# Layer 1 stores its transposed context, and layer 2 computes keys and values from it in bf16 parts and sums values in fp32

## The chip, the core and the metric

The kernel runs on one core of a Trainium2 chip. Its engines are TensorE (PE, matrix products; its weight loads are listed as PEld), VectorE (DVE), ScalarE (ACT), GpSimd (POOL) and SyncE (SP), which here does nothing but issue transfers. Each engine runs its own list of instructions in order, and they wait for one another by semaphores. The metric is the time on the device of one execution of the whole program, in microseconds (us). TensorE's clock has two levels, 1.2 and 2.4 GHz; a granted clock of 1.00 in a row is the higher one.

## The reference

Four layers work on x of 32 batches x 56 tokens x 128 features, each an attention and a feed-forward part. All four attentions read the same context, 32 x 1500 x 128. The change concerns layers 1 and 2. In layer 1, `n_all` and `m_all` of the kernel are products of these weights, so that scores are taken against the context itself:

```python
def _L1_xattn_ref(x, context, mask, Wq, Wkv, Wout, bout):     # 16 heads of 64
    k, v = jnp.split(context @ Wkv, 2, axis=-1)
    dots = jnp.einsum('bhnd,bhmd->bhnm', q, k) * SCALE - (1.0 - mask)[:, None, :, None] * MASK_NEG
    out = jnp.einsum('bhnm,bhmd->bhnd', softmax(dots), v)
```

Layer 2 has a causal self attention (called L2a in the kernel) and then an attention of its result over the 1500 context rows (L2b), both with 16 heads of 8:

```python
def _mha(xk, xv, xq, Wk, Wv, Wq, Wo, bo, masked):
    K = jnp.einsum('bse,hed->bhsd', xk, Wk)
    V = jnp.einsum('bse,hed->bhsd', xv, Wv)
    Q = jnp.einsum('bqe,hed->bhqd', xq, Wq)
    scores = jnp.einsum('bhqd,bhkd->bhqk', Q, K)
    ...
    att = jax.nn.softmax(scores / jnp.sqrt(sk), axis=-1)
    out = jnp.einsum('bhqk,bhkd->bhqd', att, V)
    ...
    return jax.nn.relu(out @ Wo + bo)
a = _mha(inputs, inputs, inputs, Wk1, Wv1, Wq1, Wo1, bo1, masked=True)
a = _layernorm(inputs + a, g1, b1)
c = _mha(context_seq, context_seq, a, Wk2, Wv2, Wq2, Wo2, bo2, masked=False)
```

## The kernel before

Constants: B = 32 batches, S = 56 tokens, H = 16 heads, HQ = 896 = 16 x 56 columns of queries, KEYS = 1500, cut into KT = 12 tiles of KP = 125 rows. A value "in bf16 parts" is stored as its bf16 rounding (high part) and the bf16 of what is left (low part); a product of two such values is taken as three bf16 products, high x high, high x low and low x high, summed in PSUM.

**Layer 1, `heads_attention` (L1487).** The batches go by pairs, a pair in 14 tiles of 128 query rows. SP (L1568 on) loads the context of a batch into one of two buffers `ctx`. PE turns it in units `keys_n` and `keys_b` (three per batch, 500 keys each); ACT copies a turned unit as bf16 into `ct_hi`, and GpSimd or DVE writes the rest into `ct_lo`. The table `PLAN` sets in which tile each unit stands: `keys_b` in tiles 0, 1 and 3, `keys_n` of the next pair in 7, 8 and 11. The transposed context in parts is thus made here, used for the scores (L1616 to L1618) and written over.

**Layer 2, self attention, `self_attention` (L2159).** Beside its own work on 56 tokens this function prepares, one batch after the other, the keys and values of the context for L2b. `UNITS` lists nine units per batch: three `turn` units (four transposes each, L2283, copied by ACT into `ctxT`), three `keys` units (one fp32 matmul of 500 columns, L2287) and three `values` units (four fp32 matmuls of 128 columns, L2291). They use two PSUM banks `L2a_u0` and `L2a_u1` in turn. Of a key or value unit ACT copies the high part (L2390), then DVE writes the low part (`rest`, L2506), and only then the bank is free. SP's list per batch is a context load (L2250), the store of the keys (L2252, 128 partitions) and that of the values (L2254, 125 partitions); there are three context buffers and two of each output. ACT waits before the first copy of a batch for the store of two batches ago. `body` writes out the order of the units among the pieces of the self attention: scores L2301, transposes L2310, weighted sums L2320, output L2329 and L2333.

**Layer 2, attention over the context, `narrow_heads_attention` (L1835), called L2b.** A batch is 12 tiles of 125 keys, and a tile has three slots. Per tile PE computes the scores of two halves of the heads (L1978, two matmuls of 224 columns each, into bank `score0` and `score1`), and the weighted sums of the tile before (`weighted`, L1994): 20 bf16 matmuls in five groups of four. The four of a group write to four different sets of 32 columns of PE (`tile_position`), one for each group of four heads; the five groups are values high x probabilities high, high x low, low x high, and a block of ones with either part, for the sums that divide the result. ACT takes the exponential of each half (L2049) as fp32; its upper 16 bits are read as the high part, and the low part is a subtraction of 125 x 896 by GpSimd (L2075) in ten tiles and by DVE (L2115) in tiles 4 and 9. There are four buffers of probabilities.

The softmax needs the maximum of every head and query over all 1500 keys ahead of the exponential. So the scores are also computed one batch ahead with the queries as rows (12 units `max`, L1959, two matmuls of 500 columns each), DVE reduces each (L2095), and the negated maxima are turned (`negmax`, L1963) and stand as further rows below the query, so that the score matmul subtracts them. The table that sets the order:

```python
MAXSLOT = (0, 3, 5, 8, 11, 13, 16, 19, 22, 24, 27, 30)
PLAN = [(MAXSLOT[n], "max", n, f"m{n % 2}", 1) for n in range(MAXU)]
PLAN += [(6, "query", 0, "u", 2), (9, "out", 0, "u", -1), (18, "negmax", 0, "u", 1), (33, "negmax", 1, "u", 1)]
```

An entry is a slot (0 to 35 of a batch), a kind, its number, the PSUM banks, and for which batch it works, counted from the current one. The maxima use two pairs of banks, `m0` and `m1`, in turn. A query (L1952) is written by ACT in four scalings, one for each head of a group (L2038), and DVE (L2087) makes its low part. `normalise` (L2123 to L2133) on DVE, after slot 1 of the next batch, reads the sums and divides. A prologue computes queries 0 and 1 and the twelve maxima of batch 0. SP loads per batch three transfers of keys and one of values, three batches deep.

## Time and profile before

| | |
|---|---|
| median of 3 runs | 4553.55 us (4531.95 to 4565.99) |
| profiled execution | 4542.79 us, span 4541.0 us |
| TensorE busy | 3775.3 us, 83% |
| VectorE busy | 2624.2 us, 58% |
| ScalarE busy | 1900.2 us, 42% |
| GpSimd busy | 1083.1 us, 24% |
| granted TensorE clock, mean | 0.864 |
| transfers | 229.33 MB, mean 51 GB/s |

These shares are means over the whole span, in which stages with quite different limits follow each other: layer 1's attention, L2a and L2b, of which the change speaks, are three of them. The rows further down are therefore taken by stretch. All times in them are us from the span's start. A matmul's row gives its stationary operand's shape ahead of the moving one's, and matmuls overlap each other, so the distance between two starts tells the pace and the duration does not. In brackets stands how long the engine was idle ahead of the instruction, and what released it.

### The profile page before, as it was taken

How to read it: one execution, taken by the hardware profiler on the slowest of the kernel's cores; microseconds unless marked ns; L12 is line 12 of the kernel's file. 1: busy time of each engine (PE TensorE's matmuls, PEld its weight loads, DVE VectorE, ACT ScalarE, POOL GpSimd, SP SyncE). 2: the span in 40 equal slices, each digit the busy share in tenths (PEclk: the TensorE clock that was granted, in tenths of full speed). 3: DMA queues.
4: the chain of work that ended last, by engine and by line, in shares of the span. 5: the costliest groups of instructions: out<-in, count | busy, mean ns of one | idle time of the engine just before them, and what ended most of it. 6: DMA issues, size and time to landing. Idle time of an engine off the chain costs nothing. (4 is left out here: it accounts for less than half of the span.)

```text
span 4541.0 us, 85060 instructions
## 1 busy us (share of the span) xinstructions
PE 3775.3 (83%) x33810; PEld 2685.8 (59%) x33810; DVE 2624.2 (58%) x4699; ACT 1900.2 (42%) x3513; POOL 1083.1 (24%) x615
## 2 busy tenths in 40 slices
PE   6969978999999999998898957788888885346878
PEld 4644446887788877886576744555555553224544
DVE  2443335766666766675354447776667673646635
ACT  1412214555555555554254423444444441105515
POOL 0000001111111111110111104555556561005506
PEclk7979987999999999999899977876778786568979
DMA  4620000000000000000144423222222210006401
GB/s 76 129 46 34 0 20 28 22 22 16 22 15 22 15 22 22 15 15 6 59 174 168 164 100 81 69 52 69 53 62 59 67 38 6 0 15 121 83 2 30
DMA packets 150594, 229.33 MB, mean 51 GB/s; under 512 B 10295, under 2 KB 113988, under 8 KB 149956
## 3 DMA queue, kind: packets, MB, share of 16 engines
q1 hardware_dynamic: 150212, 223.91, 17.8%
q8 instruction: 280, 4.59, 0.4%
q14 instruction: 102, 0.84, 0.1%
HBM read 173.81 MB, written 50.07 MB: 49 GB/s over the span
## 5 line engine op out<-in xcount | busy, mean ns | idle before, releaser
L2075 POOL TENSOR_TENSOR L2b_plo<-L2b_p 125x896 bf16<-125x896 f32 x320 | 581.7, 1829 | 488.9 <-ACT L2b_p L2049 442.0
L1779 DVE TENSOR_SCALAR_CACHE_REDUCE L_p<-L_score,L_cols 128x1500 f32<-128x1500 f32 x224 | 398.6, 1780 | 383.6 <-PE L_score L1618 383.6
L1718 ACT CAST L_pthi<-L_pt 125x512 bf16<-125x512 f32 x672 | 350.2, 594 | 541.1 <-PE L_pt L1627 541.1
L2049 ACT ACTIVATE L2b_p<-L2b_score 125x448 f32<-125x448 f32 x768 | 389.3, 542 | 427.8 <-PE L2b_score L1978 426.2
L1638 PE MATMUL L_acc<-L_chi,L_pthi 125*128 125x128 bf16 x2688 | 462.0, 219 | 0.4 <-DVE L_attn L1799 0.4
L1640 PE MATMUL L_acc<-L_chi,L_ptlo 125*128 125x128 bf16 x2688 | 461.6, 219 | 0.0
L1639 PE MATMUL L_acc<-L_clo,L_pthi 125*128 125x128 bf16 x2688 | 461.5, 219 | 0.0
L2095 DVE TENSOR_REDUCE L2b_max<-L2b_m 112x1 f32<-112x1000 f32 x256 | 306.5, 1198 | 242.4 <-PE L2b_m L1959 240.3
L1792 DVE TENSOR_TENSOR L_ptlo<-L_pt,L_pthi 125x512 bf16<-125x512 f32 x672 | 417.9, 677 | 1.1 <-ACT L_pthi L1718 1.1
L1978 PE MATMUL L2b_score<-L2b_qst,L2b_kst 100*125 100x224 bf16 x1536 | 326.0, 324 | 85.9 <-ACT L2b_p L2049 85.1
L1702 ACT ACTIVATE L_p<-L_p,L_least 128x1500 f32<-128x1500 f32 x224 | 350.4, 1564 | 7.2 <-DVE L_p L1779 5.2
L1627 PEld LDWEIGHTS L_pt<-ident,L_p 128*125 128x125 f32 x2688 | 328.5, 188 | 31.7 <-ACT L_p L1702 1.2
L1978 PEld LDWEIGHTS L2b_score<-L2b_qst,L2b_kst 100*125 100x125 bf16 x1536 | 213.6, 170 | 223.4 <-ACT L2b_p L2049 133.0
L1627 PE MATMUL L_pt<-ident,L_p 128*125 128x128 f32 x2688 | 330.2, 273 | 0.5 <-ACT L_p L1702 0.4
L1959 PE MATMUL L2b_m<-L2b_kst,L2b_qst 96*112 96x500 bf16 x768 | 293.8, 472 | 5.2 <-DVE L2b_max L2095 4.7
L1994 PE MATMUL L2b_acc<-L2b_p,L2b_vin 125*32 125x224 bf16 x3072 | 223.1, 310 | 71.7 <-DVE L2b_plo L2115 55.3
L1616 PE MATMUL L_score<-L_cthi,L_qhi 128*128 128x500 bf16 x672 | 255.6, 380 | 21.6 <-issue 13.7
L1638 PEld LDWEIGHTS L_acc<-L_chi,L_pthi 125*128 125x128 bf16 x2688 | 263.9, 98 | 0.6 <-DVE L_attn L1799 0.6
L1639 PEld LDWEIGHTS L_acc<-L_clo,L_pthi 125*128 125x128 bf16 x2688 | 263.1, 98 | 1.4
L1640 PEld LDWEIGHTS L_acc<-L_chi,L_ptlo 125*128 125x128 bf16 x2688 | 262.7, 98 | 0.0
L1617 PE MATMUL L_score<-L_ctlo,L_qhi 128*128 128x500 bf16 x672 | 253.9, 378 | 0.0
L1618 PE MATMUL L_score<-L_cthi,L_qlo 128*128 128x500 bf16 x672 | 253.5, 377 | 0.0
(548 smaller groups left out, 7276.2 us busy)
## 6 DMA issues: line engine op xcount, KB each, us to landing
L2b_kst<-L_keys SPq DMA_DIRECT2D x96, 375.0 KB, 5.6
L_ctx<-dram_ctx SPq DMA_DIRECT2D x32, 750.0 KB
L2a_ctx<-dram_ctx SPq DMA_DIRECT2D x32, 750.0 KB
L_keys<-L2a_kout SPq DMA_DIRECT2D x32, 750.0 KB, 19.6
L_values<-L2a_vout SPq DMA_DIRECT2D x32, 750.0 KB
L2b_vin<-L_values SPq DMA_DIRECT2D x32, 750.0 KB
L0x_ctx<-dram_ctx SPq DMA_DIRECT2D x32, 672.0 KB
L3x_ctx<-dram_ctx SPq DMA_DIRECT2D x32, 672.0 KB
```

The costliest lines, as they stand in the source:

```text
L1627: m = pe.transpose(pt_ps[j][0:KP, t * 128:(t + 1) * 128], probs[k % 2][:, (4 * j + t) * KP:(4 * j + t + 1) * KP], c["ident"][:, :])
L1638: pe.matmul(acc, pt_hi[k % 2][:, t, :], c_hi[half][:, t, :], start=(t == 0), stop=False)
L1639: pe.matmul(acc, pt_hi[k % 2][:, t, :], c_lo[half][:, t, :], start=False, stop=False)
L1640: m = pe.matmul(acc, pt_lo[k % 2][:, t, :], c_hi[half][:, t, :], start=False, stop=(t == KT - 1))
L1702: act.activation(probs[k % 2][:, :], probs[k % 2][:, :], ACT.Exp, bias=least[:, k:k + 1], scale=-1.0, accum_out=total[:, k:k + 1]).then_in ...
L1718: act.copy(pt_hi[k % 2][:, 4 * j:4 * j + 4, :], pt_ps[j][0:KP, :].rearrange("p (t q) -> p t q", t=4)).then_inc(hi_done, 1)
L1779: dve.tensor_scalar(probs[k % 2][:, :].rearrange("p (i n) -> p i n", i=3), score_ps[:, :].rearrange("p (i n) -> p i n", i=3)[:, :, 0:500], ...
L1792: dve.tensor_tensor(pt_lo[k % 2][:, 4 * j:4 * j + 4, :], pt_ps[j][0:KP, :].rearrange("p (t q) -> p t q", t=4), pt_hi[k % 2][:, 4 * j:4 * j ...
L1978: m = pe.matmul(score_ps[half][0:KP, (g % 2) * GW:(g % 2 + 1) * GW], k_stack[b % RK][:, g, t * KP:(t + 1) * KP], q_top[b % RK][:, g * GW:( ...
L2049: act.activation(probs[t % RP][:, half * 2 * GW:(half + 1) * 2 * GW], score_ps[half][0:KP, 0:2 * GW], ACT.Exp).then_inc(exp_done, 1)
L2075: pool.tensor_tensor(p_lo[t % RP][:, :], probs[t % RP][:, :], p_hi[t % RP], ALU.subtract).then_inc(lo_pool, 1)
L2095: dve.tensor_reduce(max3[:, p, 0:1], v, AX.XY, ALU.max).then_inc(free[f], 1)
```

## The change

**Layer 1.** `ct_hi` and `ct_lo` become the two halves of one buffer, and SP stores it, 128 partitions x 3000 bf16, once per batch into a new DRAM tensor `L1_ct`. ACT waits for that store before it writes the buffer again. The context loads are written out around the stores.

```diff
-        ct_hi = [sp_.sb(f"{name}_cthi{i}", [128, KEYS], BF16) for i in range(2)]
-        ct_lo = [sp_.sb(f"{name}_ctlo{i}", [128, KEYS], BF16) for i in range(2)]
+        ct = [sp_.sb(f"{name}_ct{i}", [128, 2, KEYS], BF16) for i in range(2)]
+        ct_hi, ct_lo = [t[:, 0, :] for t in ct], [t[:, 1, :] for t in ct]
...
+                def store(b, buf, units_done):
+                    sp.wait_ge(unit_free, units_done)
+                    sp.dma_start(ct_dram[b], ct[buf][:, :, :]).then_inc(ct_stored[buf], 16)
+                def second(p, base, first=False):
+                    store(2 * p + 1, 1, base + place("keys_b", 2, first) + 1)
+                def third(p, base, first=False):
+                    store(2 * p + 2, 0, base + place("keys_n", 2, first) + 1)
...
-                with sp.Fori(1, PAIRS) as pair:
-                    sp.wait_ge(ctx_split, 4 * pair - 2)
-                    load(2 * pair, 0)
-                    sp.wait_ge(ctx_split, 4 * pair)
-                    load(2 * pair + 1, 1)
...
+                with sp.Fori(1, PAIRS - 2) as p:
+                    second(p, unit_base(p))
+                    sp.wait_ge(ctx_split, 4 * p + 4)
+                    load(2 * p + 3, 1)
+                    third(p, unit_base(p))
+                    sp.wait_ge(ctx_split, 4 * p + 6)
+                    load(2 * p + 4, 0)
...
+                            if k == 0:
+                                wait(act, ct_stored[buf], 16 * (p + 1 - buf))
```

**Layer 2, self attention.** It loads the stored transposed context instead of the context, so the three `turn` units are gone, and the weights are split into bf16 parts once. A key unit is three bf16 matmuls of 500 columns, a value unit twelve bf16 matmuls of 128 columns. Values are stored as fp32 by one copy of ACT, without DVE; keys are stored in parts as before. The load of batch b + 3 is issued behind the two stores of batch b.

```diff
-        UNITS = [("turn", 0), ("turn", 1), ("keys", 0), ("turn", 2), ("keys", 1), ("values", 0), ("keys", 2),
-                 ("values", 1), ("values", 2)]
+        UNITS = [("keys", 0), ("values", 0), ("keys", 1), ("values", 1), ("keys", 2), ("values", 2)]
...
+        ct = [sp_.sb(f"{name}_ct{k}", [128, 2, KEYS], BF16) for k in range(RC)]
...
-                    if b + RC < B:
-                        sp.wait_ge(*freed(b, UNITS.index(("turn", 2))))
-                        sp.dma_start(ctx[b % RC][:, :, :], ctx_dram[b + RC]).then_inc(ctx_loaded[b % RC], 16)
                     sp.wait_ge(*freed(b, UNITS.index(("keys", 2))))
                     sp.dma_start(k_dram[b], k_out[b % 2][:, :, :]).then_inc(k_stored[b % 2], 16)
                     sp.wait_ge(*freed(b, UNITS.index(("values", 2))))
-                    sp.dma_start(v_dram[b], v_out[b % 2][:, :, :]).then_inc(v_stored[b % 2], 16)
+                    sp.dma_start(v_dram[b], v_out[b % 2][:, :]).then_inc(v_stored[b % 2], 16)
+                    if b + RC < B:
+                        sp.dma_start(ct[b % RC][:, :, :], ct_dram[b + RC]).then_inc(ct_loaded[b % RC], 16)
...
+                    if kind == "keys":
+                        ps, third = u_ps[f][:, 0:TK], slice(j * TK, (j + 1) * TK)
+                        pe.matmul(ps, cw_hi[:, 0, :], t_hi[:, third], start=True, stop=False)
+                        pe.matmul(ps, cw_hi[:, 0, :], t_lo[:, third], start=False, stop=False)
+                        m = pe.matmul(ps, cw_lo[:, 0, :], t_hi[:, third], start=False, stop=True)
...
+                            ps, tile = u_ps[f][0:KP, t * D:(t + 1) * D], slice((4 * j + t) * KP, (4 * j + t + 1) * KP)
+                            pe.matmul(ps, t_hi[:, tile], cw_hi[:, 1, :], start=True, stop=False)
+                            pe.matmul(ps, t_hi[:, tile], cw_lo[:, 1, :], start=False, stop=False)
+                            m = pe.matmul(ps, t_lo[:, tile], cw_hi[:, 1, :], start=False, stop=True)
```

ACT's and DVE's part of a unit (ACT now has six copies per batch where it had nine, DVE three subtractions where it had six):

```diff
-                    act.copy(out_part(kind, j, b, 0), unit_part(kind, f)).then_inc(hi_done, 1)
+                    if kind == "keys":
+                        act.copy(key_part(j, b, 0), u_ps[f][:, 0:TK]).then_inc(hi_done, 1)
+                    else:
+                        act.copy(v_out[b % 2][:, j * 4 * D:(j + 1) * 4 * D], u_ps[f][0:KP, 0:4 * D]).then_inc(u_free[f], 1)
...
-                    dve.tensor_tensor(out_part(kind, j, b, 1), unit_part(kind, f), out_part(kind, j, b, 0), ALU.subtract
+                    dve.wait_ge(hi_done, 3 * b + j + 1)
+                    dve.tensor_tensor(key_part(j, b, 1), u_ps[f][:, 0:TK], key_part(j, b, 0), ALU.subtract
                                       ).then_inc(u_free[f], 1)
```

PE's list for one batch of L2a begins before like this (L2301 are the scores of the self attention, L2283 turns, L2310 its transposes, L2287 keys, L2320 its sums, L2291 values):

```order
L2301 MATMUL L2a_s<-L2a_kall,L2a_qown 112x56 x4
L2283 MATMUL L2a_u<-ident,L2a_ctx 128x125 x4
L2301 MATMUL L2a_s<-L2a_kall,L2a_qown 112x56 x4
L2283 MATMUL L2a_u<-ident,L2a_ctx 128x125 x4
L2310 MATMUL L2a_t<-ident,L2a_p 56x112 x4
L2287 MATMUL L2a_u<-L2a_ctxT,L2a_cwk 128x500
L2310 MATMUL L2a_t<-ident,L2a_p 56x112 x4
L2283 MATMUL L2a_u<-ident,L2a_ctx 128x125 x4
L2320 MATMUL L2a_a<-L2a_vnow,L2a_pT 56x9 x8
L2287 MATMUL L2a_u<-L2a_ctxT,L2a_cwk 128x500
L2320 MATMUL L2a_a<-L2a_vnow,L2a_pT 56x9 x8
L2291 MATMUL L2a_u<-L2a_cwv,L2a_ctxT 125x128 x4
```

Now it begins like this (L2299, L2308 and L2318 are scores, transposes and sums; L2283 to L2285 a key unit, L2289 to L2291 one tile of a value unit, which has four such tiles in a row):

```order
L2299 MATMUL L2a_s<-L2a_kall,L2a_qown 112x56 x4
L2283 MATMUL L2a_u<-L2a_ct,L2a_cwhi 128x500
L2284 MATMUL L2a_u<-L2a_ct,L2a_cwhi 128x500
L2285 MATMUL L2a_u<-L2a_ct,L2a_cwlo 128x500
L2299 MATMUL L2a_s<-L2a_kall,L2a_qown 112x56 x4
L2289 MATMUL L2a_u<-L2a_cwhi,L2a_ct 125x128
L2290 MATMUL L2a_u<-L2a_cwlo,L2a_ct 125x128
L2291 MATMUL L2a_u<-L2a_cwhi,L2a_ct 125x128
```

The last three rows come four times for a value unit. Behind them stand the eight transposes L2308 together, a key unit, the eight sums L2318, a value unit and so on, so that every key unit is followed by a value unit of twelve matmuls, where single turns and keys stood before. SP's list for a batch was:

```order
L2250 DMA L2a_ctx<-dram_ctx 125x1536
L2252 DMA L_keys<-L2a_kout 128x3000
L2254 DMA L_values<-L2a_vout 125x3072
```

It now is:

```order
L2249 DMA L_keys<-L2a_kout 128x3000
L2251 DMA L_values<-L2a_vout 125x1536
L2253 DMA L2a_ct<-L_ct 128x3000
```

The load has moved behind the stores, has 128 partitions in place of 125, and the values store has half as many elements of twice the size.

**Layer 2, attention over the context.** Values and probabilities enter the weighted sums as fp32: a tile has eight matmuls, in two groups of four, and no low part is computed. One exponential per tile reads two banks, and the scores have two pairs of banks, which alternate by tile. The maxima have one pair of banks, and their slots move. The query is copied and scaled once by ACT and spread over the heads by three operations of GpSimd.

```diff
+    MAXSLOT = (0, 2, 5, 7, 10, 12, 15, 17, 20, 22, 25, 27)
+    PLAN = [(MAXSLOT[n], "max", n, "m", 1) for n in range(MAXU)]
+    PLAN += [(6, "query", 0, "u", 2), (9, "out", 0, "u", -1), (18, "negmax", 0, "u", 1), (32, "negmax", 1, "u", 1)]
...
+        PROLOGUE.append(("max", n, "m", 0))
...
-        unit_ps = {"u": sp_.ps(f"{name}_u"), "m0": sp_.ps(f"{name}_m0", 1024), "m1": sp_.ps(f"{name}_m1", 1024)}
-        score_ps = [sp_.ps(f"{name}_score{k}") for k in range(2)]
+        unit_ps = {"u": sp_.ps(f"{name}_u"), "m": sp_.ps(f"{name}_m", 1024)}
+        score_ps = [sp_.ps(f"{name}_score{k}", 1024) for k in range(2)]
...
-                            pe.wait_ge(*freed("query", 0, n))
+                            pe.wait_ge(q_step, 3 * n + 3)
...
-                    t, half = divmod(s, 2)
...
-                    wait(pe, exp_done, HALVES * b + s - 1)
+                    wait(pe, exp_done, KT * b + t - 1)
...
-                        m = pe.matmul(score_ps[half][0:KP, (g % 2) * GW:(g % 2 + 1) * GW],
+                        m = pe.matmul(score_ps[t % 2][0:KP, half * 512 + (g % 2) * GW:half * 512 + (g % 2 + 1) * GW],
...
+                    if half:
+                        m.then_inc(scores_full, 1)
...
-                    terms = [(0, hi, 0), (0, lo, 0), (1, hi, 0), (None, hi, 1), (None, lo, 1)]
-                    for n, (w, p, x) in enumerate(terms):
+                    pe.wait_ge(exp_done, KT * b + t + 1)
+                    for x in range(2):
                         for g in range(G):
-                            v = v_one[:, :] if w is None else v_in[b % RK][:, w, t, 32 * g:32 * g + 32]
+                            v = v_one[:, :] if x else v_in[b % RK][:, t, 32 * g:32 * g + 32]
                             m = pe.matmul(acc_ps[32 * g:32 * g + 32, x * GW:(x + 1) * GW], v,
-                                          p[:, g * GW:(g + 1) * GW], start=(t == 0 and n == 0),
+                                          probs[t % RP][:, g * GW:(g + 1) * GW], start=(t == 0 and x == 0),
                                           stop=(t == KT - 1), skip_group_check=True, tile_position=(0, 32 * g))
                     m.then_inc(av_done, 1)
```

ACT and GpSimd in L2b (the two `q_parts` loops of ACT and DVE and the subtractions of GpSimd and DVE are gone; of GpSimd's three operations the first is shown, the others round it to bf16 and subtract for the low part):

```diff
-                        for h in range(4):
-                            out, q = q_parts(n, h)
-                            m = act.activation(out, q, ACT.Copy, scale=own_q[0:96, h:h + 1])
-                        m.then_inc(q_hi, 1)
+                        wait(act, q_step, 3 * n)
+                        act.activation(q_raw[:, :], ps[0:96, 0:G * S], ACT.Copy, scale=scale).then_inc(free[f], 1)
...
+                    act.activation(probs[t % RP][:, :].rearrange("k (h n) -> k h n", h=2),
+                                   score_ps[t % 2][0:KP, :].rearrange("k (h n) -> k h n", h=2)[:, :, 0:2 * GW],
                                    ACT.Exp).then_inc(exp_done, 1)
...
+                    pool.tensor_tensor(
+                        q_wide[:, :].rearrange("r (g h s) -> r g h s", g=G, h=4),
+                        q_raw[:, :].rearrange("r (g o s) -> r g o s", g=G, o=1).broadcast_to([96, G, 4, S]),
+                        own[0:96, :].rearrange("r (o h u) -> r o h u", o=1, u=1).broadcast_to([96, G, 4, S]),
+                        ALU.mult).then_inc(q_step, 1)
```

PE's list in L2b from the first scores of batch 0 on was (L1978 scores, L1959 maxima of the next batch, L1994 weighted sums):

```order
L1978 MATMUL L2b_score<-L2b_qst,L2b_kst 125x224 x6
L1959 MATMUL L2b_m<-L2b_kst,L2b_qst 112x500 x2
L1978 MATMUL L2b_score<-L2b_qst,L2b_kst 125x224 x4
L1959 MATMUL L2b_m<-L2b_kst,L2b_qst 112x500 x2
L1978 MATMUL L2b_score<-L2b_qst,L2b_kst 125x224 x2
L1994 MATMUL L2b_acc<-L2b_p,L2b_vin 32x224 x4
L1994 MATMUL L2b_acc<-L2b_plo,L2b_vin 32x224 x4
L1994 MATMUL L2b_acc<-L2b_p,L2b_vin 32x224 x4
L1994 MATMUL L2b_acc<-L2b_p,L2b_vone 32x224 x4
L1994 MATMUL L2b_acc<-L2b_plo,L2b_vone 32x224 x4
L1959 MATMUL L2b_m<-L2b_kst,L2b_qst 112x500 x2
L1978 MATMUL L2b_score<-L2b_qst,L2b_kst 125x224 x2
```

It now is (L1996 scores, L1978 maxima, L2011 weighted sums, L1971 a query):

```order
L1996 MATMUL L2b_score<-L2b_qst,L2b_kst 125x224 x6
L1978 MATMUL L2b_m<-L2b_kst,L2b_qst 112x500 x2
L1996 MATMUL L2b_score<-L2b_qst,L2b_kst 125x224 x2
L1978 MATMUL L2b_m<-L2b_kst,L2b_qst 112x500 x2
L1996 MATMUL L2b_score<-L2b_qst,L2b_kst 125x224 x4
L2011 MATMUL L2b_acc<-L2b_p,L2b_vin 32x224 x4
L2011 MATMUL L2b_acc<-L2b_p,L2b_vone 32x224 x4
L1978 MATMUL L2b_m<-L2b_kst,L2b_qst 112x500 x2
L1996 MATMUL L2b_score<-L2b_qst,L2b_kst 125x224 x2
L1971 MATMUL L2b_u<-hT,L2b_wq 96x56 x4
L1996 MATMUL L2b_score<-L2b_qst,L2b_kst 125x224 x2
```

The second maximum now stands behind one pair of score matmuls, without weighted sums between it and the first, and a tile's weighted sums are two rows in place of five.

**What both share:** the values in DRAM are now fp32.

```diff
-        v_dram = nc.dram_tensor("L2_values", [B, KP, 2, KT * D], BF16, kind="Internal").ap()
+        v_dram = nc.dram_tensor("L2_values", [B, KP, KT * D], F32, kind="Internal").ap()
```

## Rows read from the trace of the kernel before

**Rows 1.** Busy by stretch: length, PE, PEld, DVE, ACT, POOL (instructions), clock, share, GB/s.
```profile
690.00:2130.00 1440.00, 1374.65 (x14399) 1144.49 (x14400) 973.75 (x1743) 810.88 (x1345) 187.50 (x64) 0.98 0.05 19
...
2245.00:2672.00 427.00, 388.02 (x3131) 302.68 (x3129) 202.38 (x359) 209.45 (x425) 54.62 (x58) 0.96 0.42 167
...
2750.00:3765.00 1015.00, 836.22 (x10323) 535.29 (x10322) 710.94 (x809) 435.68 (x919) 581.75 (x320) 0.76 0.22 58
```

**Rows 2.** Timeline of the DMA queue in L2a: start us, issuing us, line, transfer.
```profile
2300.78 0.34 SPq L2252 DMA_DIRECT2D L_keys<-L2a_kout  x1
...
2645.54 0.34 SPq L2252 DMA_DIRECT2D L_keys<-L2a_kout  x1
```

**Rows 3.** Waits in L2a, 2300 to 2600 us: total us, times, longest us.
```profile
ACT L2a_vout L2390 <- DMA L_values<-L2a_vout: 45.1, 16, 3.7
```

**Rows 4.** Two stretches: a context load (layer 1), a key store (L2a).
```profile
1010.00:1012.00 2.00, 2.00 (x26) 2.00 (x26) 0.81 (x2) 0.29 (x2) 0.00 (x0) 1.00 0.32 135
2670.00:2672.00 2.00, 0.87 (x5) 0.44 (x4) 1.15 (x3) 1.05 (x3) 0.00 (x0) 1.00 0.82 339
```

**Rows 5.** Timeline of one L2b tile, full clock: start us, us, engine, instruction.
```profile
3024.08 0.41 PE L1978 MATMUL L2b_score<-L2b_qst,L2b_kst 100*125 100x224 bf16 x2
3024.32 0.59 PE L1959 MATMUL L2b_m<-L2b_kst,L2b_qst 96*112 96x500 bf16 x2
3024.75 0.35 PE L1978 MATMUL L2b_score<-L2b_qst,L2b_kst 100*125 100x224 bf16 x2
3024.95 1.20 DVE L2095 TENSOR_REDUCE L2b_max<-L2b_m 112x1 f32<-112x1000 f32 x1 [0.16 <-PE L2b_m L1959]
3025.03 0.28 PE L1994 MATMUL L2b_acc<-L2b_p,L2b_vin 125*32 125x224 bf16 x4
...
3025.64 0.41 PE L1978 MATMUL L2b_score<-L2b_qst,L2b_kst 100*125 100x224 bf16 x2
```

**Rows 6.** Timeline of L2b: DVE, ACT, and idle PE in brackets.
```profile
3006.23 0.62 DVE L2123 TENSOR_TENSOR L2b_picked<-L2b_acc,L2b_own 128x448 f32<-128x448 f32 x1
...
3008.56 1.19 DVE L2095 TENSOR_REDUCE L2b_max<-L2b_m 112x1 f32<-112x1000 f32 x1
3009.07 1.45 ACT L2038 ACTIVATE L2b_qst<-L2b_u,L2b_ownq 96x224 bf16<-96x224 f32 x4 [2.72 <-PE L2b_u L1952]
...
3010.99 0.41 PE L1978 MATMUL L2b_score<-L2b_qst,L2b_kst 100*125 100x224 bf16 x2 [1.97 <-ACT L2b_p L2049]
...
3030.00 0.38 PE L1994 MATMUL L2b_acc<-L2b_p,L2b_vin 125*32 125x224 bf16 x4 [1.78 <-DVE L2b_plo L2115]
...
2741.92 2.31 DVE L2095 TENSOR_REDUCE L2b_max<-L2b_m 112x1 f32<-112x1000 f32 x2 [0.20 <-PE L2b_m L1959]
...
2743.17 2.18 PE L1959 MATMUL L2b_m<-L2b_kst,L2b_qst 96*112 96x500 bf16 x4 [0.46 <-DVE L2b_max L2095]
```

**Rows 7.** Timeline of L2a: the three kinds of units on PE.
```profile
2403.35 2.01 PE L2291 MATMUL L2a_u<-L2a_cwv,L2a_ctxT 128*125 128x128 f32 x16 [1.71 <-DVE L2a_vout L2506]
...
2408.15 1.02 PE L2287 MATMUL L2a_u<-L2a_ctxT,L2a_cwk 128*128 128x500 f32 x2
...
2409.39 0.59 PE L2283 MATMUL L2a_u<-ident,L2a_ctx 125*128 125x125 f32 x4
```

**Rows 8.** Timeline of layer 1: bf16 matmuls of 128 columns, one after the other.
```profile
1002.49 0.22 PE L1638 MATMUL L_acc<-L_chi,L_pthi 125*128 125x128 bf16 x1
1002.55 0.22 PE L1639 MATMUL L_acc<-L_clo,L_pthi 125*128 125x128 bf16 x1
```

**Rows 9.** Timeline of layer 3: fp32 matmuls on two halves of the columns.
```profile
4263.13 2.73 PE L1000 MATMUL L3x_s<-L3x_ctxT,L3x_qpad 128*64 128x500 f32 x12
...
4263.60 0.14 PEld L1000 LDWEIGHTS L3x_s<-L3x_ctxT,L3x_qpad 128*64 128x64 f32 x2 [0.28 <-issue]
```

**Rows 10.** Lines of L2b: count, busy us, mean ns, idle before and releasers.
```profile
L2075 POOL TENSOR_TENSOR L2b_plo<-L2b_p 125x896 bf16<-125x896 f32 x320 | 581.7, 1829 | 488.9 <-ACT L2b_p L2049 442.0 <-PE L2b_acc L1994 46.8
L2049 ACT ACTIVATE L2b_p<-L2b_score 125x448 f32<-125x448 f32 x768 | 389.3, 542 | 427.8 <-PE L2b_score L1978 426.2
```

218 lines of the change are left out of this document (91 added, 127 removed).

## The prediction

> **What bounds the kernel now.** I read the table by stretches first, then the waits, single stretches of the timeline, and the lines. Layer 1's attention [rows 1] keeps TensorE (PE) busy for 1374.65 of 1440 us; the change adds there one store per batch and touches no instruction on PE. The store goes on SP's queue ahead of a context load and waits for the last third of the turned context, written at slot 3 or 11 of the 14 tiles of a pair (1440 / 16 = 90 us, 6.4 a tile); the load behind it is next read 11 or 10 tiles later, over 60 us, and the DMA share is 0.05. ACT waits for the store only when it writes the same buffer again, a pair later. So layer 1 costs nothing here. Two stretches are left.
>
> In layer 2's self attention (L2a, 427 us, 32 batches) PE is busy 388.02 us, 12.1 per batch. Yet its key stores are issued (2645.54 - 2300.78) / 26 = 13.26 us apart [rows 2], 26 periods between the two rows shown. The other 1.2 us come from the transfers: ScalarE (ACT) waits 45.1 us in 300 us for the store of the values two batches back [rows 3]. A 768,000-byte transfer thus takes 5.7 us in the first form and at most 2.3 in the second, and a batch has two of the first (context in, values out) and one of the second: 13.7 us of the five engines' time, about the period. L2a is bound by DMA, with PE 1.2 us behind.
>
> In the narrow attention (L2b, 1015 us, 31.7 per batch) PE is busy 836.22 us, so idle 5.6 per batch, at a mean clock of 0.76. At full clock a tile costs 1.56 us, from scores to scores [rows 5]: 0.24 scores A, 0.43 maxima M, 0.28 scores B, 0.61 weighted sums W. Twelve tiles are 18.7; a query, an output and two turned maxima add 1.4 (small terms, read from the timeline without a row here): 20.1 us. The remaining 31.7 - 5.6 - 20.1 = 6.0 us are what the 1.2 GHz level costs. Its level falls after idle stretches such as the two in [rows 6]: 1.97 us behind ACT, whose four query scalings hold up an exponential, and 1.78 us behind VectorE's (DVE) split.
>
> **The change, L2a.** Per batch it removes three units of four transposes: (0.59 - 0.27) / 3 = 0.107 us each [rows 7], 1.28 us. A key unit goes from two fp32 passes, 0.42 apart in a group of 1.02, to three bf16 matmuls of 500 columns at the 0.21 of M's two [rows 5]: 0.84 to 0.63, three times: -0.63. A value unit goes from eight fp32 passes, (2.01 - 0.27) / 15 = 0.116 each [rows 7], 0.93 us, to twelve bf16 matmuls. Their cost no row shows: stationary 125 columns, moving 128. From below it is 0.056 each [rows 8], with 128 stationary columns; from above 0.12, the pace of the scores, with the same 125 stationary columns and 224 moving [rows 5]. I take 0.11, nearer the row with the same stationary width: 1.3 us, +0.37 a unit, +1.1 a batch. PE: 12.1 - 1.28 - 0.63 + 1.1 = 11.3 us.
>
> The Trainium skill, TensorE: Matmul & The Clock Gate, sections "LDWEIGHTS" and "Weight-path perf modes", speaks for the slow end: a weight load takes columns / 1.2 ns, and the fast load needs exactly 128 of them. By it a value matmul costs 104 ns and PE 11.2 us a batch; by [rows 8] alone it would be 9.4. No run here shows this shape yet.
>
> DMA: the context load becomes a 128-partition one (2.3), the values store keeps 125: 5.7 + 2.3 + 2.3 = 10.3 us, no longer the bound. ACT loses three of nine copies, DVE three of six subtractions; both are under PE. With 0.2 us for what is not hidden the period is 11.5: (11.5 - 13.26) x 32 = **-56 us**. Bounds: 10.3 (-95) if the weight load is hidden, 12.1 (-37) if PE gains nothing.
>
> **The change, L2b.** W: 20 bf16 matmuls in five groups of four become eight fp32 ones, two passes each, in four groups of four. Layer 3 has six fp32 matmuls over 500 columns, which take the left and the right half of PE's columns in turn: their 12 passes last 2.73 us, not 12 x 0.42, and weight loads come two at a time [rows 9], so two passes run side by side. For 224 columns that is 0.19. If all four column groups run together, as the bf16 ones do, W = 4 x 0.19 + 0.10 = 0.86, +0.25 a tile, +3.0 a batch: 23.1 us of work. If only the two shown do, it is rival B.
>
> The splits leave: GpSimd's 1.83 us for ten tiles [rows 10] and DVE's for two, and with them the wait of 1.78. The query's four scalings become one copy, which ends the wait of 1.97. The rest of the query, three operations on 96 partitions, goes to GpSimd, which is then otherwise empty: 3 x 1.83 = 5.5 us by [rows 10], ten tiles (some 26 us) ahead of the maxima that wait for it. The exponentials merge: two of 0.54 [rows 10] become one of about 1 us, and scores have two tiles' banks, so ACT (12 us of 31) stays behind PE.
>
> In their place comes the single pair of banks for maxima. DVE starts 0.63 us after M starts [rows 5], and PE gets the bank 1.25 us after that (2741.92 to 2743.17) [rows 6]; M itself is 0.43, so 1.45 us of other PE work must lie between two M. With A and B 0.25 each, between slots lie: 0 to 2, 0.25, idle 1.2; 5 to 7, 1.3 with the query, idle 0.15; 10 to 12, 15 to 17 and 25 to 27, W and one score, 1.1, idle 0.35 each; 20 to 22, 0.5, idle 0.95; 12 to 15 and 22 to 25, 1.36, idle 0.1 each; the others none. From 2 to 5 DVE also normalises the batch before, 2.33 us from its start at 3006.23 to the maximum behind it [rows 6]: PE has 1.36 where 3.0 are needed, idle 1.7. Sum 5.25 us a batch, as much as now (5.6).
>
> The clock: the two waits of 1.2 and 1.7 us at the start of a batch follow each other, as idle enough as those that now bring the level down; the second fall, at the split, has no counterpart. I take 2.3 us for 6.0. Batch: 23.1 + 5.25 + 2.3 = 30.7, -1.0 x 32 = **-32 us**. Before the loop, twelve maxima for batch 0 stand in a row, now 2.4 us apart (the 0.63 becomes 1.1 at half clock, plus 1.25) for 1.16 (two maxima in 2.31) [rows 6], less what lies under the turned maxima, and the first query goes through three GpSimd operations: **+13 us**.
>
> Sum: -56 - 32 + 13 = -75. The profiled execution took 4542.79 us; the median of the three runs is 4553.55, 11 above. I apply the difference to the median: **4479 us**.
>
> **The rivals.**
> A, the forecast: 4479, own range 4440 to 4515. Chance 0.55.
> B, fp32 column groups run two at a time. For it: the run of [rows 9] uses no more than two. Against: bf16 runs four, and nothing says that width matters. W = 8 x 0.19 + 0.10 = 1.6, a tile +1.0. Work is 32.1; idle falls to 3.3 as W covers most gaps; clock 1. Batch 36.4, +150; with -56 + 13, +107: 4661, slower. It decides from W = 1.3 on, where the gain of L2a is eaten. Chance 0.2.
> C, the single bank pair costs the clock twice a batch as now: 23.1 + 5.25 + 6 = 34.4, +86; in all +43: 4597. For it: the level falls after waits of this size. Against: from slot 5 to 20 little idle is left at half clock, since PE's work there doubles. Chance 0.13.
> D, the value matmuls' weight loads are hidden: -95 for L2a, -114 in all: 4439. Chance 0.12.
>
> **How the numbers follow.** One per cent, 45 us, is about what a measurement can tell here. Faster than 4508: four fifths of A (0.43) and all of D: 0.55. Within 1%: the rest of A and half of C: 0.19. Slower: B and half of C: 0.26. The range reaches from just under D, 4435, to B's own value, 4661: below its upper end lie A, C, D and half of B.
>
> **What would show it.** L2a: period 11.5 us, no waits of ACT for the values store, DMA share still above 0.35. Its line of value matmuls tells the pace: 0.105 or 0.056. L2b: W from 0.61 to 0.86 us at full clock; waits of PE for DVE's L2b_max, now none, about 5 us a batch; GpSimd nearly idle; mean clock above 0.8. W of 1.6 would prove B; a mean clock under 0.78 C. Layer 1 changing by more than 10 us, or a queue of stores delaying its context loads, would prove the first paragraph wrong.

## The result, and the profile after

The changed kernel takes 4370.51 us (median of 4 runs, 4362.81 to 4372.03), the kernel before, run again beside it, 4558.07 us: a ratio of 0.9595, 95% interval 0.9554 to 0.9636. That is -188 us. The forecast was 4479 us, -75, with a range down to 4435: the direction was right, the size less than half of what came.

The stretches of the changed kernel, which answer to [rows 1] (same columns; layer 1, L2a, and L2b without its two ends):

```profile
690.00:2130.00 1440.00, 1374.56 (x14405) 1144.02 (x14403) 975.04 (x1745) 810.94 (x1345) 187.55 (x64) 0.98 0.10 36
2245.00:2550.00 305.00, 292.97 (x3196) 238.92 (x3195) 134.15 (x261) 153.28 (x324) 54.62 (x58) 0.93 0.61 230
2620.00:3550.00 930.00, 791.12 (x8357) 428.48 (x8358) 562.68 (x618) 350.34 (x423) 156.89 (x90) 0.93 0.24 64
```

By the first and last matmul of each stage (of layer 1 its scores, of L2a its units), the 172.6 us between the two profiled spans (4541.0 and 4368.4) lie thus:

| stage | before, us | after, us | difference | forecast |
|---|---|---|---|---|
| layer 1's attention | 1394.2 | 1392.4 | -2 | 0 |
| L2a | 430.5 | 310.6 | -120 | -56 |
| prologue of L2b | 25.6 | 37.1 | +11.5 | +13 |
| L2b, 32 batches | 1016.5 | 947.0 | -69.5 | -32 |
| all that lies between and behind | | | +7 | 0 |

**L2a.** Key stores were 13.26 us apart [rows 2]. They now come (2550.57 - 2304.83) / 25 = 9.83 us apart on the mean, not 11.5. Single periods of these 25 go from 8.70 to 13.46 us, the longest where the clock is low. Two single batches of the changed kernel, from one key store to the next, both at the full clock:

```profile
2335.95:2344.66 8.71, 8.71 (x104) 7.22 (x104) 4.34 (x8) 4.81 (x11) 1.93 (x2) 1.00 0.66 254
2423.11:2433.00 9.89, 9.10 (x106) 7.47 (x106) 4.44 (x9) 5.04 (x12) 1.93 (x2) 1.00 0.63 236
```

In the first TensorE never idles and the batch takes 8.71 us. In the second it takes 9.89, with a DMA share of 0.63, and ACT waits for a store, which answers to [rows 3] (here 2300 to 2520 us). The prediction had named the absence of this wait as one of its signs:

```profile
ACT L2a_vout L2385 <- DMA L_values<-L2a_vout: 30.4, 15, 2.9
```

The value matmuls, which [rows 8] was to bound from below, follow each other 0.058 us apart. Starts are in the first column:

```profile
2400.23 0.22 PE L2290 MATMUL L2a_u<-L2a_cwlo,L2a_ct 128*125 128x128 bf16 x1
2400.28 0.22 PE L2291 MATMUL L2a_u<-L2a_cwhi,L2a_ct 128*125 128x128 bf16 x1
2400.34 0.22 PE L2289 MATMUL L2a_u<-L2a_cwhi,L2a_ct 128*125 128x128 bf16 x1
2400.40 0.22 PE L2290 MATMUL L2a_u<-L2a_cwlo,L2a_ct 128*125 128x128 bf16 x1
```

The loads of the stationary operand have records of their own (PEld; two groups from 2400 to 2540 us, the mean ns of one in the column after the busy time):

```profile
L2291 PEld LDWEIGHTS L2a_u<-L2a_cwhi,L2a_ct 128*125 128x125 bf16 x172 | 24.5, 142 | 0.0
L2284 PEld LDWEIGHTS L2a_u<-L2a_ct,L2a_cwhi 128*128 128x128 bf16 x43 | 4.3, 100 | 0.0
```

A load of 125 columns is recorded at 0.142 us and one of 128 at 0.100. The first is longer than the distance between two value matmuls, so it lies under other matmuls.

**L2b.** A tile at the full clock, which answers to [rows 5] (columns as there):

```profile
3016.45 0.59 PE L1978 MATMUL L2b_m<-L2b_kst,L2b_qst 96*112 96x500 bf16 x2
...
3016.87 0.36 PE L1996 MATMUL L2b_score<-L2b_qst,L2b_kst 100*125 100x224 bf16 x2
...
3017.16 0.58 PE L2011 MATMUL L2b_acc<-L2b_p,L2b_vin 125*32 125x224 f32 x8
...
3017.56 0.56 PE L2011 MATMUL L2b_acc<-L2b_p,L2b_vone 125*32 125x224 f32 x8
...
3018.05 0.41 PE L1996 MATMUL L2b_score<-L2b_qst,L2b_kst 100*125 100x224 bf16 x2
```

The weighted sums W take 0.89 us (3017.16 to 3018.05), where 0.61 stood and 0.86 was forecast: four fp32 column groups run together (the first four matmuls start within 0.02 us of each other), and rival B is refuted. In their neighbourhood stand the new waits. At the head of a batch, behind the single pair of banks and DVE's normalise (the forecast had 1.2 and 1.7 us there):

```profile
3004.31 0.63 PE L1978 MATMUL L2b_m<-L2b_kst,L2b_qst 96*112 96x500 bf16 x2 [1.10 <-DVE L2b_max L2114]
...
3007.84 0.63 PE L1978 MATMUL L2b_m<-L2b_kst,L2b_qst 96*112 96x500 bf16 x2 [1.63 <-DVE L2b_max L2114]
```

TensorE's waits from 2650 to 3580 us (total, times, longest), 31.4 batches:

```profile
PE L2b_m L1978 <- DVE L2b_max L2114: 88.1, 91, 1.6
PE L2b_m L1978 <- DVE L2b_max L2116: 35.2, 57, 0.9
```

That is 3.9 us a batch for the bank of maxima, by the idle time in brackets. The brackets leave a part out. They begin at the end of the matmul before, and that end is modelled. These two rows have no bracket:

```profile
3027.49 0.41 PE L1996 MATMUL L2b_score<-L2b_qst,L2b_kst 100*125 100x224 bf16 x2
3027.96 0.63 PE L1978 MATMUL L2b_m<-L2b_kst,L2b_qst 96*112 96x500 bf16 x2
```

Yet the maximum starts 0.47 us after the pair of scores, where it took 0.24 in [rows 5]: it waited 0.23 us. Taken in this way, from start to start, the waits for this bank add to 5.0 us a batch (mean over the loop; a maximum that waits for nothing starts 0.096 us after a score matmul, and what follows the sums 0.283 us after their last).

The granted clock of L2b went from 0.76 to 0.93. Before, 482 of 1015 us lay at the 1.2 GHz level, 15.1 us a batch, in 50 separate falls in 32 batches. From 2650 to 3580 us it is now 93 of 930 us, 3.0 us a batch on the mean, in 15 falls in 31 batches: it no longer falls in every batch.

### The profile page after: what moved, and what is told of

It is laid out like the page before. It is cut to its first block and busy times, and to the rows that moved or that the text cites. A ratio compares the mean times of both kernels' runs of the same rounds, so it can differ in the third digit from the quotient of the medians.

```text
span 4368.4 us, 80698 instructions
## 1 busy us (share of the span) xinstructions
PE 3665.7 (84%) x32370; PEld 2535.4 (58%) x32370; DVE 2411.0 (55%) x4411; ACT 1778.1 (41%) x2938; POOL 668.8 (15%) x391
## 5 line engine op out<-in xcount | busy, mean ns | idle before, releaser
L2061 ACT ACTIVATE L2b_p<-L2b_score 125x896 f32<-125x896 f32 x384 | 352.0, 917 | 450.2 <-PE L2b_score L1996 447.8
L1978 PE MATMUL L2b_m<-L2b_kst,L2b_qst 96*112 96x500 bf16 x768 | 257.7, 419 | 144.3 <-DVE L2b_max L2114 99.4
L1647 PE MATMUL L_score<-L_ct,L_qhi 128*128 128x500 bf16 x672 | 254.4, 379 | 21.2 <-issue 13.2
L1996 PE MATMUL L2b_score<-L2b_qst,L2b_kst 100*125 100x224 bf16 x1536 | 265.8, 275 | 0.4 <-DVE L2b_qst L2124 0.4
L1996 PEld LDWEIGHTS L2b_score<-L2b_qst,L2b_kst 100*125 100x125 bf16 x1536 | 174.2, 140 | 140.6 <-issue 72.5
L1648 PE MATMUL L_score<-L_ct,L_qhi 128*128 128x500 bf16 x672 | 253.3, 377 | 0.0
L1649 PE MATMUL L_score<-L_ct,L_qlo 128*128 128x500 bf16 x672 | 252.9, 376 | 0.0
L2011 PE MATMUL L2b_acc<-L2b_p,L2b_vin 125*32 125x224 f32 x3072 | 235.1, 379 | 0.0
L2011 PE MATMUL L2b_acc<-L2b_p,L2b_vone 125*32 125x224 f32 x3072 | 225.8, 367 | 0.0
```

What stands on the lines that cost most here:

```text
L1996: m = pe.matmul(score_ps[t % 2][0:KP, half * 512 + (g % 2) * GW:half * 512 + (g % 2 + 1) * GW], k_stack[b % RK][:, g, t * KP:(t + 1) * KP] ...
L2011: m = pe.matmul(acc_ps[32 * g:32 * g + 32, x * GW:(x + 1) * GW], v, probs[t % RP][:, g * GW:(g + 1) * GW], start=(t == 0 and x == 0), stop ...
L2061: act.activation(probs[t % RP][:, :].rearrange("k (h n) -> k h n", h=2), score_ps[t % 2][0:KP, :].rearrange("k (h n) -> k h n", h=2)[:, :, ...
```

## The experiments

Twelve more kernels ran, each beside the kernel before. "-110" and the like are differences of medians, to the kernel before unless another is named. The kernel before had a median of 4538 to 4564 us beside them, so such a difference between runs of different groups is good to some 20 us. The stages are compared by their traces as well, one trace for each kernel. There too the same code differs from run to run: L2b of the kernel before takes 1016.5 us in its own trace and 1037.3 in that of `l2a_alone`, which has it unchanged.

### L2a alone, and L2b alone

`l2a_alone` is the changed kernel with the whole `narrow_heads_attention` of before and values in bf16 parts:

```diff
-        v_out = [sp_.sb(f"{name}_vout{k}", [KP, KT * D]) for k in range(2)]
+        v_out = [sp_.sb(f"{name}_vout{k}", [KP, 2, KT * D], BF16) for k in range(2)]
...
                         rest(b, 0)
...
+                        rest(b, 1)
...
+                        rest(b, 3)
...
+                        rest(b, 5)
```

> The change in layer 1 and in L2a alone; values stay in bf16 parts (so DVE keeps its three subtractions for values) and L2b is that of before. Theory 1, the two halves of the gain add: L2a goes from 430 us to 310 to 320 (430 to 310 in the changed kernel), the rest stays: total 4435 to 4450, -110 to -120. Rival, L2a's gain needs the values as fp32, since the two banks are held by DVE's subtraction (ACT, then DVE) and PE waits for them: then PE waits of over 1 us a batch for L2506's successor appear and L2a stays above 350 us, total above 4475.

Measured: 4454.22 us, ratio 0.9755 (0.9716 to 0.9794), -110, 4 us above the expected range. L2a takes 316.1 us, 5.5 more than in the changed kernel (whose L2a takes 310.5 to 314.6 in the runs that share it). DVE's subtractions of the values are not what held L2a, so the rival is out.

`l2b_alone` is the kernel before with the new `narrow_heads_attention`; of L2a only the values' output changes:

```diff
-                    act.copy(out_part(kind, j, b, 0), unit_part(kind, f)).then_inc(hi_done, 1)
+                    if kind == "values":
+                        act.copy(v_out[b % 2][:, j * 4 * D:(j + 1) * 4 * D], unit_part(kind, f)).then_inc(u_free[f], 1)
+                    else:
+                        act.copy(out_part(kind, j, b, 0), unit_part(kind, f)).then_inc(hi_done, 1)
```

> The change in L2b alone (values stored as fp32 by one copy of ACT; layer 1 and the keys, turns and loads of L2a as before). Theory 1: L2b 1017 to 947 us and its prologue +11.5, so -58, and L2a little changed, since it is bound by its three transfers, two of them of 125 partitions: total about 4500. Rival, DVE's subtractions of the values are what L2a waits for (the trace of before shows 1.7 us idle behind them once a batch): L2a falls by 20 us or more too, total below 4480.

Measured: 4496.43 us, ratio 0.9856 (0.9816 to 0.9896), -68, as the first theory has it. L2b with its prologue is 57 us shorter (37.0 + 947.7 for 25.6 + 1016.5), L2a stays (431.1 us). The parts add within the 20 us, -110 and -68 for -188, and each can be looked at by itself.

### What bounds L2a, before and after: the transfers of 125 partitions, cut in two

```diff
-                    sp.dma_start(v_dram[b], v_out[b % 2][:, :]).then_inc(v_stored[b % 2], 16)
+                    for p0, p1 in ((0, 112), (112, KP)):
+                        sp.dma_start(v_dram[b, p0:p1], v_out[b % 2][p0:p1, :]).then_inc(v_stored[b % 2], 16)
```

> The changed kernel with the store of the values cut in two, 112 and 13 partitions. Theory 1, after the change L2a still runs at the pace of its transfers: a period of 9.83 us where TensorE's pieces at full clock add to 8.5, with ACT waiting 30 us in 220 for the values store. Then the period falls to 8.7 to 9.0 us, L2a from 310 to 280 or 285, total -25 to -30 against the changed kernel, about 4343. Rival, DVE's and ACT's turns on the two banks set the period: the waits for the store vanish and the period stays within 0.3 us, total within 10 us of the changed kernel.

Measured: 4335.99 us, ratio to before 0.9506 (0.9483 to 0.9528), so -34 against the changed kernel by the medians. L2a falls from 310.6 to 280.4 us. All of it now looks like the one batch above that did not wait: batches of 8.71 and 8.96 us in turn, the clock at 1.00, no wait for a store. Of the 30 us, 11 are idle time of TensorE (12.0 to 1.4 us over the units) and 19 its busy time with the same matmuls (298.5 to 279.1): 42.6 us lay at the 1.2 GHz level, 1.6 do now. So the waits for the store also cost clock.

```profile
2427.55:2436.51 8.96, 8.96 (x106) 7.47 (x106) 4.53 (x9) 5.25 (x12) 1.93 (x2) 1.00 0.78 260
2300.00:2520.00 220.00, 218.64 (x2553) 180.69 (x2552) 108.14 (x208) 125.96 (x262) 43.05 (x46) 1.00 0.76 260
```

The same cut in the kernel before, for context loads and values stores:

> The kernel before with each transfer of 125 partitions in L2a (context loads, values stores) cut into 112 and 13 partitions; nothing else. Theory 1, L2a was bound by these transfers at 13.26 us a batch, and TensorE's pieces at full clock add to 11.1 us: the period falls to 11.5 to 12.2, -35 to -55 us, total about 4510. Rival, the period of before is set by the alternation of two banks among PE, ACT and DVE: no change beyond 10 us.

Measured: 4532.9 us, ratio 0.9937 (0.991 to 0.9965), -31 by the medians, a little less than expected. L2a goes from 430.5 to 406.5 us. Two batches of the kernel before, both at the full clock, and two with the cut:

```profile
2340.68:2352.79 12.11, 11.87 (x99) 9.20 (x99) 6.42 (x11) 6.54 (x14) 1.93 (x2) 1.00 0.43 176
2403.90:2417.72 13.82, 11.88 (x104) 9.34 (x103) 6.59 (x12) 6.78 (x14) 1.93 (x2) 1.00 0.43 168
```

```profile
2343.59:2355.70 12.11, 11.86 (x99) 9.20 (x99) 6.42 (x11) 6.55 (x14) 1.93 (x2) 1.00 0.57 192
2406.09:2419.99 13.90, 13.39 (x101) 10.47 (x101) 6.69 (x12) 6.92 (x15) 1.93 (x2) 0.88 0.50 167
```

Before, a batch took 12.11 us where it didn't wait and 13.82 where it did, and the cut takes the waits for the store away: over the units TensorE's idle time falls from 37.9 to 12.3 us, which is all of the gain of 24 us, 0.75 a batch. It is less than 1.6 us a batch, since only some of the batches waited, and since the clock still falls. With the cut, in three batches of every eight the granted clock is 0.88 and the batch takes 13.65 to 13.90 us, with TensorE busy for 13.39 of 13.90 us. The kernel before has such batches too, and in both L2a lies at the 1.2 GHz level for 39.2 us. So before the change the transfers bound most of L2a, as forecast, but TensorE stood close behind: with the transfers out of the way a batch takes 406.5 / 32 = 12.7 us on the mean, for 13.5.

The share is the key to the sum of the prediction: 0.32 of 16 engines for 125 partitions [rows 4]. The Trainium skill, DMA: Bandwidth & Descriptors, section "Why a DMA increments its semaphore by 16 and not by 1", says that a transfer uses the largest number of engines up to 16 that divides the slowest dimension of both its sides: by that, five for 125, 16 for 112 or 128. The trace agrees: a transfer of 125 partitions alone has a share of 0.32, which is five of 16, and with the cut the values store no longer holds anything up.

### The fp32 sums by themselves, and the subtractions by themselves

`sums_alone`: layer 1 and L2a changed; in L2b only the fp32 values, probabilities and sums. Against the changed kernel, in short:

```diff
-    MAXSLOT = (0, 2, 5, 7, 10, 12, 15, 17, 20, 22, 25, 27)
-    PLAN = [(MAXSLOT[n], "max", n, "m", 1) for n in range(MAXU)]
+    MAXSLOT = (0, 3, 5, 8, 11, 13, 16, 19, 22, 24, 27, 30)
+    PLAN = [(MAXSLOT[n], "max", n, f"m{n % 2}", 1) for n in range(MAXU)]
...
-        score_ps = [sp_.ps(f"{name}_score{k}", 1024) for k in range(2)]
+        score_ps = [sp_.ps(f"{name}_score{k}") for k in range(2)]
...
-                        act.activation(q_raw[:, :], ps[0:96, 0:G * S], ACT.Copy, scale=scale).then_inc(free[f], 1)
+                        for h in range(4):
+                            out, q = q_parts(n, h)
+                            m = act.activation(out, q, ACT.Copy, scale=own_q[0:96, h:h + 1])
```

> The changed kernel in layer 1 and L2a; in L2b only the fp32 values, probabilities and sums of the change, with the banks, slots, exponentials and query of before. Against the run of L2a alone (4454) it tells what the fp32 sums by themselves do. Theory 1: weighted sums +0.28 us a tile, 3.4 a batch, against the wait of 1.8 us for DVE's subtraction and half of the 481 us at 1.2 GHz in L2b that follow it: L2b 30 to 30.5 us a batch, -40 to -55 us, total 4400 to 4415. Rival, the gain of L2b is that of query and banks, and the sums only cost: +3.4 us less 1.8, total at or above 4480.

Measured: 4381.78 us, ratio 0.9633 (0.9577 to 0.9688), some 20 us below the expected range, with L2b's 30.25 us a batch inside it. Against `l2a_alone` that is -72 by the medians (-56 by the two ratios, each to its own chip's kernel before); by the stages L2b goes from 1037.3 to 968.0 us, 32.4 to 30.25 a batch. The theory's direction holds, and the rival is out. Although the matmuls take longer, the fp32 sums bring 69 of the 90 us that L2b's loop loses from `l2a_alone` to the changed kernel (1037.3 to 947.0); taken from the 1016.5 us of the kernel before's own trace it would be 49 of 70.

`no_splits` asks why: `l2a_alone` without the computing of the low parts, which are zeros here; the 20 bf16 matmuls stay.

```diff
-                    pe.wait_ge(lo_dve if t in DVE_TILES else lo_pool, lo_count(b, t))
+                    pe.wait_ge(exp_done, HALVES * b + 2 * t + 2)
...
-                        pool.tensor_tensor(p_lo[t % RP][:, :], probs[t % RP][:, :], p_hi[t % RP], ALU.subtract
-                                           ).then_inc(lo_pool, 1)
+                for k in range(RP):
+                    pool.memset(p_lo[k][:, :], 0.0).then_inc(lo_pool, 1)
```

> The run of L2a alone with one thing gone from L2b: the low parts of the probabilities are not computed (their buffers are filled with zeros once, so the result lacks them); the 20 bf16 matmuls a tile stay, reading those buffers, and wait for the exponential only. Against 4454 it prices what GpSimd's and DVE's subtractions cost TensorE. The fp32 sums gained 72 us there although their matmuls take 3.4 us a batch more, so this should gain about 72 + 107 = 180 if the subtractions are the whole cause: L2b from 32.4 to about 27 us a batch, its time at 1.2 GHz from 17 us a batch to under 7, total 4270 to 4310. Rival, a good part of the gain of the fp32 sums comes from their own longer and denser work holding the clock up: then less than 110 us, total above 4345.

Measured: 4302.11 us, ratio 0.9448 (0.942 to 0.9475): -152 by the medians against `l2a_alone`, within the range of theory 1, though short of its 180 (and -140 by the two ratios). L2b takes 27.6 us a batch. TensorE's longest waits (`l2a_alone` first, some 31 batches each) show that one goes and the other stays:

```profile
PE L2b_score L2012 <- ACT L2b_p L2083: 82.0, 59, 2.0
PE L2b_acc L2028 <- DVE L2b_plo L2149: 55.4, 31, 1.9
```

```profile
PE L2b_score L2012 <- ACT L2b_p L2084: 84.1, 61, 2.0
```

and the clock (`l2a_alone`, `no_splits`, `sums_alone`, `banks_back`, each a stretch inside L2b; columns as in [rows 1]):

```profile
2650.00:3650.00 1000.00, 833.08 (x9904) 531.25 (x9893) 694.28 (x790) 416.37 (x879) 558.79 (x307) 0.73 0.22 57
```

```profile
2650.00:3500.00 850.00, 718.58 (x9900) 465.82 (x9899) 598.21 (x729) 421.86 (x886) 0.00 (x0) 0.86 0.26 68
```

```profile
2650.00:3590.00 940.00, 818.81 (x8530) 462.86 (x8527) 601.52 (x733) 424.72 (x890) 0.00 (x0) 0.89 0.23 61
```

```profile
2640.00:3480.00 840.00, 749.70 (x8694) 429.84 (x8695) 554.49 (x617) 401.96 (x821) 156.97 (x90) 1.00 0.26 69
```

The subtractions cost 4.8 us a batch. The wait that goes is 1.8 of them (55.4 us in 31), but other waits grow, and TensorE's idle time falls by 1.1 us only, from 5.4 to 4.3 a batch. Its busy time falls by 3.7, from 27.0 to 23.3, with the same matmuls: that is the clock, 0.73 to 0.86, and the time at 1.2 GHz goes from 17 to 7.7 us a batch. So most of what the subtractions cost, they cost through the clock. The fp32 sums then give back 2.7 (27.6 to 30.25), near the 12 x 0.28 = 3.4 of their matmuls.

### The query, and the banks

`query_back` is the changed kernel with the query as before, `banks_back` the changed kernel with the banks, slots and half exponentials of before. The first takes the query's part of the diff of `sums_alone` above (its last four lines), the second the rest of it, with the half exponentials.

> The changed kernel with the query as before (four scalings by ACT, four operations by DVE, GpSimd empty). Theory 1, the long wait behind the query (1.97 us once a batch before) and a fall of the clock come back: 2 to 3 us a batch, total 4435 to 4470. Rival, the second pair of score banks hides the scalings: within 15 us of the changed kernel.

Measured: 4423.12 us, ratio 0.972 (0.966 to 0.978), +53 by the medians against the changed kernel; L2b 30.8 us a batch for 29.6. The cost lies between the theory and its rival. No score matmul waits for an exponential here, where in `sums_alone`, with one bank for each half, such waits add to 82.6 us in 940: the second pair of score banks hides part of ACT's scalings.

> The changed kernel with the PSUM banks of before in L2b: two pairs for maxima and their old slots, one bank for each half of the scores and two exponentials a tile; fp32 sums and the query by GpSimd stay. Theory 1, the one pair of banks costs L2b 4.4 us of idle TensorE a batch (the waits for DVE's maxima add to 133 us in 930) and nearly all of its 92 us at 1.2 GHz: then L2b loses most of both, 29.6 to 26 or 27 us a batch, its prologue 11 us, total 4260 to 4290 against 4370. Rival, the merged exponential with its second score bank was needed: score matmuls wait for ACT (85 us in the kernel before) and the batch stays at 29 us or more, total at or above 4355.

Measured: 4264.97 us, ratio 0.9374 (0.932 to 0.9428), -106 against the changed kernel, as the first theory has it. L2b takes 26.7 us a batch with the clock at 1.00 (row above), the prologue 25.0 us. So the swap of banks for one larger exponential cost the change 106 of the 294 us that the rest of it gains.

Against `sums_alone` (4382), with the same banks, the query alone is worth 117 us; between `query_back` and the changed kernel, with the banks swapped, it is 53. The two edits are not independent, by the waits just named.

`slots_spread` keeps the single pair and moves its slots:

```diff
-    MAXSLOT = (0, 2, 5, 7, 10, 12, 15, 17, 20, 22, 25, 27)
+    MAXSLOT = (3, 6, 7, 9, 11, 14, 17, 20, 23, 26, 28, 31)
...
-    PLAN += [(6, "query", 0, "u", 2), (9, "out", 0, "u", -1), (18, "negmax", 0, "u", 1), (32, "negmax", 1, "u", 1)]
+    PLAN += [(6, "query", 0, "u", 2), (9, "out", 0, "u", -1), (26, "negmax", 0, "u", 1), (35, "negmax", 1, "u", 1)]
```

> The changed kernel with another table in L2b: maxima at slots 3, 6, 7, 9, 11, 14, 17, 20, 23, 26, 28, 31, turned maxima at 26 and 35. A count of the changed kernel by its own durations (a bank is free 1.87 us after its matmuls start, normalise takes 2 us ahead of the maxima) gives 4.7 us of idle a batch for its table and 3.0 for this one. Theory 1: -1.7 us a batch, and as much again at most from the clock: total 4290 to 4320. Rival, the last turned maximum stands right ahead of the next batch's first scores, and its chain (DVE, TensorE, DVE) costs what the rest gains: total within 15 us of 4370.

Measured: 4296.32 us, ratio 0.9443 (0.9388 to 0.9498), -74 against the changed kernel: 27.3 us a batch, 2.3 less. The count gave 1.7 for the waits, and taken from start to start they fall by 1.5 (5.0 to 3.5). The clock stays at 1.00 here, where 3.0 us a batch lay at 1.2 GHz, and that can give the rest.

```profile
2660.00:3510.00 850.00, 758.07 (x8596) 424.81 (x8592) 560.12 (x617) 356.45 (x435) 154.19 (x89) 1.00 0.26 67
```

### A version faster than both

In `banks_back` TensorE still waits twice a batch for an exponential (from 2640 to 3480 us):

```profile
PE L2b_score L1996 <- ACT L2b_p L2061: 52.5, 62, 0.9
```

The timeline shows why: the half exponential stands in ACT's queue behind the copy of the query, which waits for the query's matmuls.

```profile
3013.50 0.81 PE L1971 MATMUL L2b_u<-hT,L2b_wq 128*96 128x56 f32 x8
...
3014.34 0.35 ACT L2052 ACTIVATE L2b_qraw<-L2b_u 96x224 f32<-96x224 f32 x1 [3.08 <-PE L2b_u L1971]
3014.60 0.96 ACT L2061 ACTIVATE L2b_p<-L2b_score 125x448 f32<-125x448 f32 x2
...
3015.18 0.40 PE L1996 MATMUL L2b_score<-L2b_qst,L2b_kst 100*125 100x224 bf16 x2 [0.87 <-ACT L2b_p L2061]
```

With the exponential first:

```diff
                         exps(b, t, 0)
-                        slot(b, 3 * t)
                         exps(b, t, 1)
+                        slot(b, 3 * t)
```

> The changed kernel with the banks of before in L2b, the values store cut into 112 and 13 partitions, and on ACT both exponentials of a tile ahead of the query's or the output's copy. Theory: the two waits for an exponential behind those copies (0.87 and 0.83 us a batch in the run with the banks of before) go, -1.5 us a batch or -45 us; the split store gives -34: total 4265 - 34 - 45 = 4186, range 4175 to 4235. Rival, the copies then free the bank of queries and outputs later, and TensorE waits there instead: 4225 or more.

It is `banks_back` with this edit and the cut of the values store.

Measured: 4168.21 us, ratio 0.9158 (0.9133 to 0.9183), 7 us below the expected range. L2a gives 30 us, as in `after_split`. L2b goes from 26.7 to 24.7 us a batch, 2.0 less where the brackets promised 1.5. From start to start they agree: the score pair behind the query starts 0.65 us after it for 1.68, the one behind the output's matmuls 0.18 for 1.17, together 2.0.

The next moves three slots (the expectation speaks of the last six maxima, of which these three are moved):

```diff
-    MAXSLOT = (0, 3, 5, 8, 11, 13, 16, 19, 22, 24, 27, 30)
+    MAXSLOT = (0, 3, 5, 8, 11, 13, 16, 19, 21, 24, 26, 29)
```

> As the run before it, with the maxima from the sixth on one or two slots sooner (16, 19, 21, 24, 26, 29 in place of 16, 19, 22, 24, 27, 30). Theory: the wait of 0.49 us a batch for the last negated maximum goes: -10 to -15 us. Rival, two maxima follow each other too closely for DVE (1.2 us each) and PE waits for a bank: no gain.

Measured: 4157.48 us, ratio 0.914 (0.9115 to 0.9166), -11 us against `best1` and -213 against the changed kernel by the medians. The gain is in the expected range, though the wait for the negated maximum has not gone: it fell from 0.5 to 0.3 us a batch. L2a takes 280.4 us, L2b 784 us, 24.5 a batch, TensorE busy for 96% of it:

```profile
2600.00:3370.00 770.00, 736.88 (x8651) 427.65 (x8650) 558.09 (x620) 395.84 (x817) 157.11 (x90) 1.00 0.29 76
```

### Why the scores seemed slow

> The changed kernel with the score matmuls of L2b over 128 rows in place of 100 (28 rows of ones against zeros; same result, same 125 stationary and 224 moving columns). It asks why those take 0.12 us each, twice what the value matmuls of L2a take with the same 125 stationary columns (0.058) and 128 moving. Theory 1, moving columns set the pace (0.215 for 500, 0.058 for 128) and the scores' extra is a turn of their own, of weights or banks: nothing moves, pairs stay at 0.24 to 0.25, total within 10 us of 4370. Rival, a stationary operand of 100 rows is loaded more slowly than one of 125 or 128 rows: a pair falls to about 0.20, 1.0 us a batch, -25 to -35 us in all.

```diff
-        k_stack = [sp_.sb(f"{name}_kst{k}", [R, G, KEYS], BF16) for k in range(RK)]
+        k_stack = [sp_.sb(f"{name}_kst{k}", [128, G, KEYS], BF16) for k in range(RK)]
-        q_top = [sp_.sb(f"{name}_qst{k}", [R, HQ], BF16) for k in range(RK)]
+        q_top = [sp_.sb(f"{name}_qst{k}", [128, HQ], BF16) for k in range(RK)]
```

(Rows 100 to 127 hold ones in the first and zeros in the second.) Measured: 4360.6 us, ratio 0.9604 (0.9569 to 0.9638), the same as the changed kernel within the intervals. The rows loaded are not the reason. The trace of the changed kernel has the answer in another place: how long a pair of scores lasts depends on what stands around it.

```profile
3004.78 0.55 PE L1996 MATMUL L2b_score<-L2b_qst,L2b_kst 100*125 100x224 bf16 x4
3005.25 0.59 PE L2011 MATMUL L2b_acc<-L2b_p,L2b_vin 125*32 125x224 f32 x8
...
3020.25 0.63 PE L1978 MATMUL L2b_m<-L2b_kst,L2b_qst 96*112 96x500 bf16 x2 [0.20 <-DVE L2b_max L2114]
3020.72 0.36 PE L1996 MATMUL L2b_score<-L2b_qst,L2b_kst 100*125 100x224 bf16 x2
3020.91 0.26 PE L1982 MATMUL L2b_u<-ident,L2b_negmax 112*100 112x112 f32 x1
3021.01 0.35 PE L1996 MATMUL L2b_score<-L2b_qst,L2b_kst 100*125 100x224 bf16 x2
3021.30 0.59 PE L2011 MATMUL L2b_acc<-L2b_p,L2b_vin 125*32 125x224 f32 x8
```

The pair at 3020.72 is followed by a single small matmul 0.19 us later, 0.095 each; the pair at 3021.01 by the weighted sums 0.29 us later; and four scores ahead of the sums take 0.47, so that two more cost 0.18 or 0.19. By the single starts of this trace at full clock, a score matmul follows another after 0.096 us. The changes to and from the sums cost more: 0.187 from the last score to the sums, and 0.147 from the first score behind them to the second. In [rows 5] the first pair of a tile is 0.147 + 0.096 = 0.24 and the second 0.098 + 0.187 = 0.28. So the 0.12 held some 0.05 or 0.09 us of changing over, which is not a pace.

## Why the prediction was wrong in size

- **Layer 1 costs nothing: right.** 1392.4 us for 1394.2, at a DMA share of 0.10 for 0.05.
- **L2a was bound by its transfers: right, and so was their sum.** Forecast 13.7 us for three transfers, measured 13.82 at the full clock; for the changed ones 10.3 against 9.9. Wrong was that they would no longer bound it: ACT still waits 30.4 us in 220 for the values store. But they bound only part of the batches: while a context is loaded ahead, or after a stretch at 1.2 GHz in which the transfers caught up, batches run at TensorE's 8.8, and the mean over the stage, 9.7, came below the lower bound that I had set at 10.3.
- **The cost of a value unit: the step that failed.** "I take 0.11, nearer the row with the same stationary width". It is 0.058, so twelve matmuls are 0.69 us and not 1.3. Taken from start to start, changing over included, the three value units of one batch (the kernel before from 2340.68 us) went from 3.26 to 2.28 us: -0.98 where +1.1 was forecast. With 0.058 in the prediction's own sum TensorE needs 9.5 us a batch, the transfers' 10.3 become the period, and L2a gives -95 us instead of -56: 39 of the 64 us that were missed there. The row I leaned on, the scores of [rows 5], held a pair and the change to the next kind; read as a pace it is a quarter too high even for its own 224 columns (0.12 for 0.095). Rival D had this cost right, at a chance of 0.12. What the Trainium skill says there (TensorE: Matmul & The Clock Gate, sections "LDWEIGHTS" and "Weight-path perf modes", a load of columns / 1.2 ns and a fast one for exactly 128) would give 0.104 us a matmul, if the load set the pace. The trace agrees in that the loads of 125 columns are longer than those of 128 (0.142 and 0.100 us in the rows above), and not in the pace: 0.058 us a matmul.
- **The rest of TensorE's batch in L2a: half the size.** Key units went from 3.15 to 2.11 us (-1.04 for -0.63), turns left with 1.40 (for 1.28), since a short group costs more than its matmuls: a key unit 0.70 us, its three matmuls at 0.215 only 0.645. With the values that is -3.4 us a batch, from 12.2 to 8.8, where -0.8 was forecast. The 25 us that are left of the miss in L2a are the transfers (9.9 for 10.3, 13 us) and the batches that run at TensorE's pace.
- **L2b, the weighted sums: right** (0.89 for 0.86).
- **L2b, the single pair of banks: right.** Forecast 5.25 us of waiting a batch, measured 5.0 from start to start. Slot by slot, at the full clock:

| slot of the maximum | 2 | 5 | 7 | 12 | 15 | 17 | 22 | 25 | 27 |
|---|---|---|---|---|---|---|---|---|---|
| forecast, us | 1.2 | 1.7 | 0.15 | 0.35 | 0.1 | 0.35 | 0.95 | 0.1 | 0.35 |
| measured, us | 1.26 | 1.70 | 0.42 | 0.23 | 0.03 | 0.27 | 1.07 | 0.03 | 0.23 |

- **L2b, the clock: too dear, the second term that was mis-sized.** 29.6 less 23.5 of work (twelve tiles of 1.84 and 1.4) and 5.0 of waits leaves 1.1 us where 2.3 was forecast; 3.0 us at half speed can cost 1.5 at most. In sum 23.5 + 5.0 + 1.1 for 23.1 + 5.25 + 2.3: a miss of 1.05 us a batch, 34 us, and the clock is more than all of it. The forecast let the two waits at the head of a batch bring the level down each time; it fell in about every second batch.
- **The prologue: right**, 11.5 for 13.
- **Rivals.** B is out (W 0.89). C is out (a mean clock of 0.93). D was the right mechanism for L2a, but its floor of 10.3 us a batch was too high and its total of 4439 is still 69 us above the result.

What stays open: why the clock falls in `before_split` in three of eight batches, with TensorE busy 96 to 98% of the time, and stays up in `after_split`; and why the two waits at the head of an L2b batch bring it down only every second time. No run relieves TensorE in L2a and leaves its transfers as they were. And which of its parts makes the query worth 117 us with one set of banks and 53 with the other was not taken apart further.

## What to carry to other kernels

Take the price of a matmul from a run of several of its own kind, never from the distance to the next kind: that distance can hold the changing over, which for short matmuls is as long as they are. Take a wait from start to start too, against the same pair where nothing waits: the idle time that a profile names is less by the modelled end of the matmul before (3.9 for 5.0 us a batch here). When a stage is bound twice over (here transfers at 13.8 us, TensorE at 12.2), relieving one gains the difference at most (-24 us in L2a for the transfers alone); a change that relieves both, as this one did, gains more (-120). And look in a change for the part that gives back what the others win: undone by itself, the bank swap was worth more than half of what the whole change had gained.

## What the runs showed of the hardware

- A bf16 matmul of 128 columns against 128 x 125 stationary elements starts 0.058 us after the one before it, twelve in a row, although a load of its weights is recorded at 0.142 us (0.100 for 128 columns).
- Score matmuls of 224 columns start 0.096 us apart in a row. From the last of them to the weighted sums on four sets of 32 columns it is 0.187, and from the first behind those sums to the second 0.147.
- Eight fp32 passes of 224 columns in four sets of 32 columns take 0.40 us; the four sets run together.
- A transfer of 125 partitions moved 135 GB/s at a share of 0.32, one of 128 partitions 339 at 0.82. Cut into 112 and 13, the values store no longer held up L2a, which then moved 260 GB/s at 0.76.
- In L2b the clock sat at 1.2 GHz for 15.1 us of each batch before, for 3.0 on the mean in the changed kernel and not at all from 2640 to 3480 us with the banks of before. When a wait of 1.8 us went there, TensorE's idle time fell by 1.1 us a batch and its busy time by 3.7.
- The granted clock fell in a stretch in which TensorE was busy for 13.39 of 13.90 us.
